# The router's second product from two tiles stacked on the partitions, in a two-layer graph-attention and expert kernel

## The reference, cut to what matters

```python
x = x + L0_gnn(layernorm(x), adj)      # attention over 128 nodes, elu
x = x + L0_ffn(layernorm(x))           # 6 experts, three layers each, top 2 by the router
x = x + L1_gnn(layernorm(x), adj)
x = x + L1_ffn(layernorm(x))           # 8 experts, router on the mean of each graph
```

```python
rh = relu(features @ router_w1 + router_b1)              # 128 -> 64
expert_logits = softmax(rh @ router_w2 + router_b2)      # 64 -> 6
top_w, top_i = top_k(expert_logits, 2)
routing_weights = softmax(top_w)
```

## Time and profile before

| | us |
|---|---|
| median of three runs | 580.34 |
| lowest and highest of them | 580.0, 581.66 |
| the profiled execution, its own time | 581.19 |
| its span in the trace | 579.4 |

### The profile page before, as it was taken

The page is one execution under the profiler, slowest core; times in us unless marked ns, Lnnn a source line. Parts: engine busy times, 40 slices in busy tenths (PEclk is TensorE's granted clock), DMA queues, the critical chain, the costliest instruction groups (busy, mean ns, idle before and its releaser), DMA issues.

```text
span 579.4 us, 14977 instructions
## 1 busy us (share of the span) xinstructions
PE 545.0 (94%) x3752; PEld 450.9 (78%) x3784; DVE 447.9 (77%) x1656; ACT 417.6 (72%) x1097; POOL 231.0 (40%) x449
## 2 busy tenths in 40 slices
PE   7768999999999999999999999999988999999993
PEld 6555677777778877878777777877766799999993
DVE  3766869888898978989889898786556387777777
ACT  1354667878888787887878878786664678888883
POOL 6112224343433434234442433413323045666664
PEclk9898999999999999999999999999998799999998
DMA  8504135051340504315052250311320477887732
GB/s 201 124 16 150 59 106 157 10 165 45 121 145 18 164 20 145 109 55 164 2 162 95 69 164 1 109 56 57 110 74 2 132 223 232 245 249 216 226 114 72
DMA packets 78833, 66.44 MB, mean 115 GB/s; under 512 B 9916, under 2 KB 64460, under 8 KB 78796
## 3 DMA queue, kind: packets, MB, share of 16 engines
q1 hardware_dynamic: 65562, 60.60, 34.2%
q10 hardware_dynamic: 13234, 5.42, 3.4%
HBM read 61.57 MB, written 4.42 MB: 114 GB/s over the span
## 4 chain that ended last, share of the span: by engine, by line
PE 80%; issue 5%; DVE 5%; POOL 4%; ACT 3%; ACTq 1%; DMA 1%; DVEq 0%; SPq 0%; POOLq 0%
PE bank L1553 14%; PE bank L1540 13%; PE wide L206 5%; PE bank L1835 5%; PE bank L1845 4%; PE wide L1835 4%; PE wide L1845 4%; PE wide L239 4%; PE bank L1532 3%; PE bank L1533 3%; PE bank L1534 3%; PE wide L231 2%; PE wide L1581 2%; PE wide L199 2%; PE wide L220 2%
## 5 line engine op out<-in xcount | busy, mean ns | idle before, releaser
L1553 PE MATMUL bank<-w,h2w 128*128 128x128 f32 x768 | 105.1, 280 | 2.6 <-DVE h2w L1120 2.6
L1553 PEld LDWEIGHTS bank<-w,h2w 128*128 128x128 f32 x768 | 95.5, 193 | 7.9 <-DVE h2w L1120 4.1
L1540 PE MATMUL bank<-h,w 128*128 128x512 f32 x192 | 99.7, 601 | 0.3 <-ACT h L836 0.3
L831 ACT ACTIVATE h<-bank,b 128x512 f32<-128x512 f32 x96 | 66.2, 690 | 43.6 <-PE bank L1540 43.4
L836 ACT ACTIVATE h<-bank,b 128x512 f32<-128x512 f32 x96 | 66.0, 687 | 12.9 <-PE bank L1534 12.5
L1120 DVE TENSOR_TENSOR h2w<-h,wide_w 128x512 f32<-128x512 f32 x96 | 64.8, 677 | 8.7 <-ACT h L831 8.5
L1532 PE MATMUL bank<-xnTh,w1h 128*128 128x512 f32 x96 | 67.3, 701 | 0.0
L100 POOL TENSOR_TENSOR route_var_eps<-route_mean_var,eps 128x4 f32<-128x4 f32 x17 | 10.6, 625 | 119.5 <-DVE route_mean_var L93 119.4
L100 POOL TENSOR_TENSOR at_var_eps<-at_mean_var,eps 128x4 f32<-128x4 f32 x32 | 12.0, 376 | 92.4 <-DVE at_mean_var L93 92.4
L268 ACT ACTIVATE at_pr<-at_lk,at_nm 128x128 f32<-128x128 f32 x124 | 40.0, 415 | 1.7 <-DVE at_nm L303 1.5
L1533 PE MATMUL bank<-xnTh,w1l 128*128 128x512 f32 x96 | 37.9, 395 | 0.0
(11 more groups left out here) (300 smaller groups left out, 1367.8 us busy)
## 6 DMA issues: line engine op xcount, KB each, us to landing
wide_w<-w_scratch SPq DMA_DIRECT2D x96, 256.0 KB, 4.4
mask<-in_L_ffn_W SPq DMA_DIRECT2D x124, 128.0 KB, 2.5
x<-in_x SPq DMA_DIRECT2D x16, 256.0 KB, 5.1
adj_in<-in_adj SPq DMA_DIRECT2D x16, 256.0 KB, 5.7
wide_w<-bmix_scratch SPq DMA_DIRECT2D x16, 256.0 KB, 3.8
xin<-in_x SPq DMA_DIRECT2D x15, 256.0 KB, 5.5
out<-at_pr ACTq DMA_DIRECT2D x8, 256.0 KB, 3.2
out<-at_prT ACTq DMA_DIRECT2D x7, 256.0 KB, 3.0
```

The costliest lines, as they stand in the source:

```text
L831: a.activation(h2[:, e % 2, :], b_h2[:, :], ACT.Relu, bias=b2[:, e:e + 1]).then_inc(h2_ready, 1)
L1540: pe.matmul(b_h2[:, :], w2[:, e, :], h1[:, e % 2, :], start=True, stop=True).then_inc(l2_done, 1)
L1553: last = pe.matmul(b_out[:, s], h2w[:, e % 2, s], w3[:, e, :], start=False, stop=(e == E0 - 1), skip_group_check=True)
```

## The change

The four tiles of a group are now worked as two halves of two tiles. rw1h and rw1l hold the router's first weights twice, side by side, so that the hidden layer's three products fill all 128 partitions of b_misc with the same 64 rows twice. The relu takes columns 0 to 255 from the upper copy into partitions 0 to 63 of rh, and columns 256 to 511 from the lower copy into partitions 64 to 127; rh is 128 partitions by 256 columns. rw2 is 128 by 12, zero but for two blocks of 64 by 6. So two products with 128 columns of rh stationary and 12 columns moving give the logits of all four tiles, product q the tiles q and 2 + q. The second bias is no longer in the product: it is spread over 128 partitions at the start (rb2), and DVE adds it as the first step of `route_first`, which puts the tiles back in order (lgb). ROUTE goes from 13 to 14, and the counts that others wait for shift by one. The memset of the ones is gone; a memset of rw2 on GpSimd is new, and ACT waits for it before its small DMAs, of which there are two more.

```diff
-    rw1h = sb("rw1h", [P, RH], F32R)
-    rw1l = sb("rw1l", [P, RH], F32R)
-    rb1 = sb("rb1", [RH, 1])
-    rh = sb("rh", [RH + 1, GW])
-    rw2 = sb("rw2", [RH + 1, E0])
+    rw1h = sb("rw1h", [P, 2 * RH], F32R)
+    rw1l = sb("rw1l", [P, 2 * RH], F32R)
+    rb1 = sb("rb1", [2 * RH, 1])
+    rh = sb("rh", [2 * RH, GW // 2])
+    rw2 = sb("rw2", [2 * RH, 2 * E0])
+    rb2 = sb("rb2", [P, E0])
+    lgb = sb("lgb", [P, GG, E0])
...
+            p.memset(rw2[:, :], 0.0).then_inc(b3_zero, 1)
...
-                a.dma_start(rb1[:, :], A["L0_ffn_router_b1"].unsqueeze(1)).then_inc(small_loaded, 16)
-                a.dma_start(rw2[0:RH, :], A["L0_ffn_router_w2"]).then_inc(small_loaded, 16)
-                a.dma_start(rw2[RH:RH + 1, :], A["L0_ffn_router_b2"].unsqueeze(0)).then_inc(small_loaded, 16)
+                a.wait_ge(b3_zero, 1)
+                for q in range(2):
+                    half = slice(q * RH, (q + 1) * RH)
+                    a.dma_start(rb1[half, :], A["L0_ffn_router_b1"].unsqueeze(1)).then_inc(small_loaded, 16)
+                    a.dma_start(rw2[half, q * E0:(q + 1) * E0], A["L0_ffn_router_w2"]).then_inc(small_loaded, 16)
+                a.dma_start(rb2[:, :], A["L0_ffn_router_b2"].partition_broadcast(P)).then_inc(small_loaded, 16)
...
-                    a.activation(rh[0:RH, :], b_misc[0:RH, :], ACT.Relu, bias=rb1[:, :]).then_inc(rh_ready, 1)
+                    for q in range(2):
+                        half = slice(q * RH, (q + 1) * RH)
+                        part = a.activation(rh[half, :], b_misc[half, lane[q]], ACT.Relu, bias=rb1[half, :])
+                    part.then_inc(rh_ready, 1)
...
-                v.memset(rh[RH:RH + 1, :], 1.0).then_inc(split_step, 1)
+                twice = h2[:, 0, 0:RH].unsqueeze(1).broadcast_to([P, 2, RH])
...
-                lg = b_misc[:, 0:GG * E0].rearrange("p (t e) -> p t e", t=GG)
-                v.tensor_reduce(lgmx[:, :], lg, AX, ALU.max).then_inc(route_step, 1)
+                lg = b_misc[:, 0:GG * E0].rearrange("p (q h e) -> p h q e", q=2, h=2)
+                v.tensor_tensor(lgb[:, :, :].rearrange("p (h q) e -> p h q e", h=2), lg,
+                                rb2[:, :].unsqueeze(1).unsqueeze(1).broadcast_to([P, 2, 2, E0]), ALU.add)\
+                    .then_inc(route_step, 1)
                 v.wait_ge(route_step, base + 1)
+                v.tensor_reduce(lgmx[:, :], lgb[:, :, :], AX, ALU.max).then_inc(route_step, 1)
...
-                for t in range(GG):
-                    last = pe.matmul(b_misc[:, t * E0:(t + 1) * E0], rh[:, t * P:(t + 1) * P], rw2[:, :],
-                                     start=True, stop=True)
+                for q in range(2):
+                    last = pe.matmul(b_misc[:, q * 2 * E0:(q + 1) * 2 * E0], rh[:, q * P:(q + 1) * P], rw2[:, :],
+                                     start=True, stop=True, skip_group_check=True)
```

More of the change, by code:

```diff
@@ L29 @@
 SLOTS = 6
-ROUTE = 13
+ROUTE = 14
 SLOT = 2 * GG
@@ L545, in build @@
     RAW = 16 * 2
-    SMALL = 16 * 10
+    SMALL = 16 * 12
     LATE = 16 * 9
@@ L637, in _ @@
             load(1, 1)
-            sp.wait_ge(b3_zero, 1)
+            sp.wait_ge(b3_zero, 2)
             for q in range(3):
@@ L1079, in split_w1 @@
                 v.wait_ge(raw_loaded, RAW)
-                v.memset(rh[RH:RH + 1, :], 1.0).then_inc(split_step, 1)
+                twice = h2[:, 0, 0:RH].unsqueeze(1).broadcast_to([P, 2, RH])
                 raw = h1[:, :, :].rearrange("p a f -> p (a f)")[:, 0:E0 * P]
                 v.tensor_copy(w1h[:, :], raw).then_inc(split_step, 1)
-                v.tensor_copy(rw1h[:, :], h2[:, 0, 0:RH]).then_inc(split_step, 1)
-                v.wait_ge(split_step, 3)
+                v.tensor_copy(rw1h[:, :].rearrange("p (q c) -> p q c", q=2), twice).then_inc(split_step, 1)
+                v.wait_ge(split_step, 2)
                 v.tensor_tensor(w1l[:, :], raw, w1h[:, :].bitcast(F32), ALU.subtract).then_inc(split_step, 1)
-                v.tensor_tensor(rw1l[:, :], h2[:, 0, 0:RH], rw1h[:, :].bitcast(F32), ALU.subtract)\
+                v.tensor_tensor(rw1l[:, :].rearrange("p (q c) -> p q c", q=2), twice,
+                                rw1h[:, :].bitcast(F32).rearrange("p (q c) -> p q c", q=2), ALU.subtract)\
                     .then_inc(split_step, 1)
@@ L1135, in route_rank @@
                 v.tensor_reduce(psum_[:, :], pe0[:, :, :], AX, ALU.add).then_inc(route_step, 1)
-                v.wait_ge(route_step, base + 3)
+                v.wait_ge(route_step, base + 4)
                 v.reciprocal(prc[:, :], psum_[:, :]).then_inc(route_step, 1)
-                v.wait_ge(route_step, base + 4)
+                v.wait_ge(route_step, base + 5)
                 v.scalar_tensor_tensor(pd[:, :, :], pe0[:, :, :], -1.0,
@@ L1144, in route_rank @@
                     .then_inc(route_step, 1)
-                v.wait_ge(route_step, base + 6)
+                v.wait_ge(route_step, base + 7)
                 mine = lifted[:, :, :].unsqueeze(3).broadcast_to([P, GG, E0, E0])
@@ L1164, in route_weights @@
                     .then_inc(route_step, 1)
-                v.wait_ge(route_step, base + 10)
+                v.wait_ge(route_step, base + 11)
                 v.tensor_reduce(qsum[:, :], pqs[:, :, :], AX, ALU.add).then_inc(route_step, 1)
-                v.wait_ge(route_step, base + 11)
+                v.wait_ge(route_step, base + 12)
                 v.reciprocal(qrc[:, :], qsum[:, :]).then_inc(route_step, 1)
-                v.wait_ge(route_step, base + 12)
+                v.wait_ge(route_step, base + 13)
                 need(v, wrow_done, g)
@@ L1572, in route_hidden @@
                 pe.wait_ge(xnTl_ready, g + 1)
-                pe.matmul(b_misc[0:RH, :], rw1h[:, :], xnTh[:, par, :], start=True, stop=False)
-                pe.matmul(b_misc[0:RH, :], rw1l[:, :], xnTh[:, par, :], start=False, stop=False)
-                pe.matmul(b_misc[0:RH, :], rw1h[:, :], xnTl[:, par, :], start=False, stop=True)\
+                pe.matmul(b_misc[:, :], rw1h[:, :], xnTh[:, par, :], start=True, stop=False)
+                pe.matmul(b_misc[:, :], rw1l[:, :], xnTh[:, par, :], start=False, stop=False)
+                pe.matmul(b_misc[:, :], rw1h[:, :], xnTl[:, par, :], start=False, stop=True)\
                     .then_inc(rh_done, 1)
@@ L1668, in body @@
                     pe.wait_ge(small_loaded, SMALL)
-                    pe.wait_ge(split_step, 5)
+                    pe.wait_ge(split_step, 4)
                 if i0 == 0:
-                    pe.wait_ge(split_step, 12)
+                    pe.wait_ge(split_step, 11)
                 if run and i0 > 0:
```

19 lines of the change are left out of this document (10 added, 9 removed).

## The result

| | before | after |
|---|---|---|
| median of six runs, us | 580.78 | 591.83 |
| lowest and highest, us | 580.0, 581.66 | 589.31, 592.93 |
| profiled execution and its span, us | 581.19, 579.4 | 591.71, 590.0 |

The ratio is 1.0186, with a 95% interval of 1.017 to 1.0202: slower by 1.9%. The medians differ by 11.05 us, the two profiled spans by 10.6. The forecast had the sign and not the size; 591.83 lies far above the range of 580.9 to 585.0.

What follows compares the result with a forecast made beforehand. The prediction took TensorE as the bound, with ACT's run reaching the transposes at the same point. Relu +2.1, round 14 -0.45 and start +0.9 gave +2.55 us on the 580.34 median: 582.9 us, range 580.9 to 585.0.

Steps and rivals of the forecast that it cites:

- Who comes second: At at0's probability transposes, ACT's exps arrive together with TensorE, so TensorE's 0.45 us saving becomes a wait in rounds 0 to 13.
- round 14: Last round making logits, with no at0 exps behind them: only there TensorE's saving is kept, -0.45 us.
- The wait of the weight load: TensorE's load for at0's probability transposes would wait about 0.6 us for ACT's exps in rounds 0 to 13.
- The term of the relu: Router's relu on ACT, two instructions for one: 0.15 us more in each of fourteen rounds, +2.1 us (1.5 to 2.8).
- The start: Two more small DMAs issued by ACT before its first copy: +1.26 us if plain, taken as +0.9 (bounds 0 and 1.4).
- VectorE: Added bias addition of about 0.21 us falls into DVE's 1.75 us idle wait for ACT's logit exp: cost 0.
- The sum: Whole kernel: relu +2.1, round 14 -0.45, start +0.9, together +2.55 us.

Runs made afterwards that it cites:

- e3: Kernel before the change with two of the four logit products left out, relu unchanged; round 24.51 us for 24.54, whole 584.77 us.
- v1: Changed kernel with the hidden layer stacked by six 256-column products, so one 128 x 256 relu replaces the pair; round 24.33 us, whole 580.98 us.
- v4: Changed kernel with the router's relu pair one place earlier on ACT, ahead of expert 2's second relu; round 24.14 us, whole 582.45 us, ratio 1.004.
- e8: Kernel before the change with the router's relu one place earlier on ACT, ahead of expert 2's second relu; round 24.54 us.
- e1: Kernel before the change with the router's relu split into two 64 x 256 instructions, both on partitions 0 to 63; round 24.65 us, whole 586.19 us.
- e2: Kernel before the change with the hidden layer made twice and one undivided 512-column relu on partitions 64 to 127; round 24.79 us, whole 584.52 us.
- e6: Kernel before the change with two more DMAs on ACT's queue, each spreading 24 bytes to 128 partitions (256 pieces more); whole 581.95 us.
- e5: Kernel before the change with two more DMAs on ACT's queue, each one row of 24 bytes (2 pieces more); whole 581.29 us.
- v7: v5 with ten filler products instead of twenty ahead of the head's routing sums; 577.52 us, ratio 0.9926 to the kernel before the change.
- v5: Changed kernel with one stacked 128 x 256 relu, placed earlier on ACT, and router DMAs behind ACT's first copy; 574.81 us, ratio 0.9909.

## Why the prediction was right or wrong

- **Who comes second: right.** L231 stands behind ACT's run and the run starts at the end of L1554. e3 shows the saving gone into the wait, v1 shows the round following ACT's run one for one (-0.21), v4 and e8 show that TensorE is the other bound at the same point. The logits' four pairs take 0.44, and round 14 kept its 0.45. The wait of the weight load, forecast as 0.6 us, is 0.76, and the round 24.93 for 24.7: both are long by the next term.
- **The term of the relu: mis-sized, the step "Fourteen rounds at 0.15 are +2.1".** It measured 5.28 from round 0 to 14, 0.38 a round. The rows behind the 0.15 were sound, and e1 gives 0.15 for a split on the same partitions. I took the pair's halves as alike and did not ask what their different partitions do; e2 shows that as 0.29 on ACT and 0.25 in the round. The rows I drew the bounds from are splits whose parts keep the same partitions, and a bound for this case was missing. 3.18 us of the miss lie here.

 By the Trainium skill, page "ScalarE: Activation LUTs", section "What ACT_TABLE_LOAD costs", back-to-back activations overlap by about 93 ns. The relus in the earlier trace rows do, by about 0.1; in e2 they do not overlap at all with an instruction that has another first partition, so there the measurement decides against the page.
- **The start: mis-sized, the step "1.26, and a little for some 250 more descriptors in the queue".** It counted issues, and these it sized rightly: the two more are 1.23 in the changed kernel. I took 0.9 because I thought that they might partly vanish in the stall of the last issue, and that stall grew instead, by 1.67 with the issue ahead of it. The "little" for the descriptors was 0.14 in my bound, and e6 against e5 shows 2.4 for 254 pieces more. The stall of 1.70 in the earlier trace rows fits a queue that was already held up before the change, which no run shows by itself. 2.16 us of the miss (3.06 for 0.9). The stretch from there to round 0 is 0.95 longer in the changed kernel; among the four kernels with the change's start it takes from 43.5 (v1) to 46.1 us, with falls of the clock at varying points, so that the 0.95 can't be told from that scatter.

 By the Trainium skill, page "DMA: Bandwidth & Descriptors", section "Anatomy of one DMA — SWDGE (gpsimd) path", many descriptors can be emitted before their added cost shows. The section speaks of GpSimd's path; on ACT's, in e6, some 250 of them already cost ACT 2.4 us.
- **VectorE: right in its cost of 0.** The addition takes 0.19 (158.90 to 159.09 in the timeline), and DVE still waits 1.92 for the exp behind it. That wait was to be 0.2 shorter than 1.75 and is 0.17 longer: DVE is ready 0.22 later behind the logits' load, and the exp comes 0.39 later, behind ACT's longer run.
- **The head: missing from the sum.** +1.74, which no step of mine looked at, since the change does not touch it. The traces show the clock at its lower level over the fillers and TensorE's order holding the sums behind them. v7 confirms the second by taking the wait away. The table behind v7 shows what the length goes with: the mean granted clock over the head is 0.83 before and 0.77 after, and each kernel with 0.83 or more has a head of 23.8 to 24.3 us, each with less one of 25.1 or more. Why the clock falls earlier or for longer in one execution than in another is not settled, and the edits don't sort the kernels: e8 and v1 are in the one group, e1, which touches only the loop, in the other. So it stays open whether the +1.74 belongs to the change, to where its start and rounds happen to put this stretch, or to the one execution.
- **The sum:** -0.45 as forecast, +5.28 for +2.1, +3.06 for +0.9, and +0.95, +1.74 and +0.02 that were not in it: 10.60 for 2.55, 8.05 us missed.

## What to carry to other kernels

When a saving on the busiest engine ends at a wait for another engine that is only just on time, the change is worth what it does to that other engine's run; look there for a place that takes work out of the run before touching the products. Halves on different partitions cost more than the split alone: keep neighbours on ACT on the same first partition, or lay the halves out so that one instruction over all partitions serves both. Count a DMA at the start by its pieces as well as by its issues, and put what is needed late behind the engine's first real work.

## What the runs showed of the hardware

- On ACT, relus with the same first partition start 0.57 to 0.58 us apart with a length of 0.67 to 0.69; where the first partition changes from 0 to 64 or back they start 0.71 apart, with no overlap (e2). That is 0.13 to 0.14 for each change.
- Two DMAs of 256 pieces of 24 bytes in all cost ACT's queue 2.4 us more than two DMAs of one piece each (first copy at 12.42 in e6, 10.06 in e5), and the stall shows at an issue several places later (2.75 us for the bias of the experts in e6, 2.88 for the last weights in the changed kernel).
- A relu of 128 partitions by 256 columns takes 468 ns and lets the next start after 0.36 (v1); the pair of 64 by 256 columns on two halves takes 0.96 for the same elements (the changed kernel).
- In the head the 20 fillers take 2.34 us where the granted clock is at its upper level over them (e2, e5, v1) and 4.43 where it is at its lower one (0.50 in e1, 0.52 in v5).
